# Plain attention on one Trainium2 core: where the value products stand among the score pairs

## The reference

```
x = x + _L0_attn_ref(_layernorm(x), ...)           # relative attention
h = _layernorm(f, ln1_g, ln1_b);  qkv = h @ w_qkv + b_qkv
scores = einsum('bqhd,bkhd->bhqk', q, k) / sqrt(DK)
attn = softmax(scores);  o = einsum('bhqk,bkhd->bqhd', attn, v)
f = f + o @ w_o + b_o                              # then top-2 of 8 experts
```

## Time and profile before

| what | value |
|---|---|
| time, median of 3 runs | 4359.0 us (4358.93 to 4363.57) |
| span of the profiled execution | 4340.7 us |
| plain attention with its `s` (first `s` to last evacuation) | 2216.6 to 3616 us of the span |
| TensorE, VectorE, ScalarE busy over the span | 91%, 80%, 69% |

### The profile page before, as it was taken

How to read it: one execution, slowest core, us unless ns; L and a number is a source line. 1 busy time by engine, 2 the same in 40 slices (tenths; PEclk the granted TensorE clock), 3 DMA queues, 4 the chain that set the end, 5 groups by cost and what they waited for, 6 DMA issues and landing times. The chain is left out here.

```text
span 4340.7 us, 77253 instructions
## 1 busy us (share of the span) xinstructions
PE 3962.5 (91%) x26592; PEld 2108.1 (49%) x26592; DVE 3486.0 (80%) x6304; ACT 2981.4 (69%) x5821; POOL 1446.1 (33%) x1405
## 2 busy tenths in 40 slices
PE   8699999999999999996799999999999996599997
PEld 5355555555455555544433333333333333499997
DVE  6788888888888888835688898888888872477775
ACT  4078888888788878881148888888888883266664
POOL 0356666666666666641100000000000001522232
PEclk9599999999999999998879999999999997699998
DMA  8566666666676667635652323223323303676664
GB/s 312 152 160 171 165 171 165 170 165 170 159 172 165 170 160 172 164 81 188 201 99 31 53 38 47 44 40 46 50 36 48 43 7 89 172 218 172 170 179 110
DMA packets 486195, 556.39 MB, mean 128 GB/s; under 512 B 60260, under 2 KB 426836, under 8 KB 476524
## 3 DMA queue, kind: packets, MB, share of 16 engines
q1 hardware_dynamic: 465980, 526.94, 49.1%
q0 software_dynamic: 19824, 24.52, 3.4%
HBM read 347.67 MB, written 206.76 MB: 128 GB/s over the span
## 5 line engine op out<-in xcount | busy, mean ns | idle before, releaser
L371 DVE TENSOR_REDUCE pa_pm<-pa_psA 128x2 f32<-128x1024 f32 x1024 | 1207.9, 1219 | 134.9 <-PE pa_psA L460 134.8
L1098 ACT ACTIVATE ra_p<-ra_psS 128x512 f32<-128x512 f32 x2048 | 1082.0, 606 | 315.1 <-PE ra_psS L1175 223.8
L434 ACT ACTIVATE pa_p<-pa_psS 128x512 f32<-128x512 f32 x2048 | 1063.5, 604 | 247.4 <-PE pa_psS L486 243.1
L1009 DVE TENSOR_REDUCE ra_pm<-ra_psA 128x1 f32<-128x896 f32 x1024 | 1112.7, 1087 | 147.6 <-PE ra_psA L1133 132.7
L486 PE MATMUL pa_psS<-pa_qs,pa_zs 50*128 50x512 f32 x2048 | 793.2, 464 | 77.6 <-ACT pa_p L434 64.2
L460 PE MATMUL pa_psA<-pa_zs,pa_qs 48*128 48x512 f32 x2048 | 796.7, 472 | 38.0 <-DMA pa_zs<-k_halves 17.8
L1133 PE MATMUL ra_psA<-ra_zs,ra_qs 48*128 48x512 f32 x2048 | 729.9, 450 | 19.1 <-DVE ra_pm L1011 8.4
L1175 PE MATMUL ra_psS<-ra_qs,ra_zs 50*128 50x512 f32 (+3 forms) x2176 | 699.6, 406 | 28.4 <-ACT ra_p L1098 17.9
L486 PEld LDWEIGHTS pa_psS<-pa_qs,pa_zs 50*128 50x128 f32 x2048 | 342.2, 185 | 626.0 <-ACT pa_p L434 607.0
L1206 PE MATMUL ra_psO<-ra_p,ra_vs 128*32 128x512 f32 (+3 forms) x6400 | 551.0, 449 | 0.0
L1175 PEld LDWEIGHTS ra_psS<-ra_qs,ra_zs 50*128 50x128 f32 x2176 | 350.4, 186 | 409.0 <-ACT ra_p L1098 318.4
(11 more groups left out here) (247 smaller groups left out, 4947.2 us busy)
## 6 DMA issues: line engine op xcount, KB each, us to landing
relative_rows<-ra_rst SPq DMA_DIRECT2D x128, 512.0 KB, 3.9
ra_blk<-window_rows SPq DMA_DIRECT2D x128, 512.0 KB
mo_w_raw<-ffn_W SPq DMA_DIRECT2D x58, 1024.0 KB, 5.4
ra_zs<-k_halves SPq DMA_DIRECT2D x192, 248.0 KB, 7.1
ra_dl<-relative_rows SPq DMA_DIRECT2D x128, 256.0 KB, 4.7
window_rows<-ra_pc SPq DMA_DIRECT2D x128, 256.0 KB
pa_qs<-q_halves SPq DMA_DIRECT2D x192, 128.0 KB, 6.2
pa_zs<-k_halves SPq DMA_DIRECT2D x192, 128.0 KB, 6.8
```

Source lines behind the costliest of these rows:

```text
L371: dve.reduce_max(pm[:, par, 2 * a:2 * a + 2], psA[w][:, :, :], AX.X).then_inc(s_am.h, 1)
L434: act.activation(pr[:, i % NPR, :], psS[:, slot(i), :], ACT.Exp).then_inc(s_ex.h, 1)
L1009: dve.reduce_max(pm[:, q, i, 2 * left:2 * left + 1], psA[w][:, lo:lo + 2 * G - P], AX.X).then_inc(s_far.h, 1)
L1098: act.activation(dst, psS[:, slot(i), :], ACT.Exp if kind == "E" else ACT.Copy).then_inc(s_cp.h, 1)
```

## The change

The strings that order a step are replaced by one string of two steps, an even and an odd one. The `O` of an even step stays where it was. The `O` of an odd step comes one pair later, so that five pairs and three pairs alternate between one `O` and the next. In the two steps the order on TensorE was

`a s s a O s a a s | a s s a O s a a s` and becomes `a s s a O s a a s a s s a a s | O s a`.

The turn M moves from behind the `O` of step 11 to the end of step 11. `EVAC` goes from 22 to 23: ScalarE copies the quarter (the chunk) after exponential 22 of the head, 38, 54 and 70, instead of 21, 37, 53 and 69.

```diff
-EVAC = 22
+EVAC = 23
-ORDER = "assaOsaas"
+PAIR_ORDER = ("assaOsaasassaas", "Osa")
 def body_turns():
-        for item in ORDER:
-            if item == "O" and k in (F_STEP, M_STEP):
-                out.append(("F" if k == F_STEP else "M", None))
+        for item in PAIR_ORDER[k % 2]:
+            if item == "O" and k == F_STEP:
+                out.append(("F", None))
             elif item == "a":
...
+        if k == M_STEP:
+            out.append(("M", None))
...
-                        for item in ORDER:
+                        for item in PAIR_ORDER[k % 2]:
...
-                                if k == M_STEP:
-                                    if real(t, "M", None):
-                                        released(pe, t, n - 2)
-                                        turn_m(t + 1, w)
-                                    n += 1
+                        if k == M_STEP:
+                            if real(t, "M", None):
+                                released(pe, t, n - 2)
+                                turn_m(t + 1, (PT + n) % 2)
+                            n += 1
```

## The result

The changed kernel takes 4497.7 us (median of 4 runs, 4485.8 to 4514.6), the kernel before in the same comparison 4360.9 us. The ratio is 1.0317, 95% interval 1.0293 to 1.0341: slower by 137 us. Forecast were 107 us, 4466 us, with a range up to 4485. The direction holds, and so does the wait that sets the pace; the amount is 13 us outside the range.

A forecast was written before the change was run, and what follows sets the result against it. VectorE's read of Q was to bound the new order: 8 x 5.52 + 0.85 + 1.45 + 0.50 + 0.25 = 47.2 us a head against 43.6. Thirty heads and the last two gave +107 on 4359: 4466 us, range 4435 to 4485 (from 4420 with M hidden).

The forecast's parts named there:

- What bounds the old step: Old order: a chain through TensorE and ScalarE closes each step at 2.61 us, giving a head of 43.6 us.
- Two steps 5.52 us by the wait for Q: New order: `a`5 waits until VectorE has read turn Q, so two steps take 5.52 us, not 5.22; +2.4 us a head.
- 5.08 by ScalarE's chain: Rival: the wait for Q doesn't bind, two steps take 5.08 us; 4311 us, chance 0.05.
- 0.56 over 0.43 for `a`6: Time from `a`6, right after O, to its reduction: 0.56 us as after a pause; 0.43 would give 5.46 for two steps.
- Evacuation free: ScalarE's copy of a quarter no longer delays the step: -0.10 us four times a head, -0.4.
- M +1.45: Turn M at the end of step 11: the next turn waits for S to be read, +1.45 us; before, M cost 0.10.
- last maxima +0.25: The last maxima on VectorE lengthen the gap between reductions from 1.13 to 1.36 us: +0.25 a head.
- end of head +0.50: End of a head, where `s`65 waits for exponential 63: +0.5 us, as before 0.49.
- F 0.85: Place F, gather and keep, costs 0.85 us a head as before.
- The signs: Expected in traces: VectorE hole 0.91 per two steps, O 0.43 behind `a`5, TensorE hole about 1 behind M, idle 220 to 260.
- The clock: Rival: TensorE's clock falls in the new pauses; one O in sixteen at low clock, +27, 4493 us, chance 0.03.
- What lies around the span is 18.3: Time outside the profiled span of 4340.7 us, taken as 18.3 us; so +107 was set on the median of 4359.

The follow-up runs named there:

- new_again: The changed kernel, unedited, run once more beside later variants on the same chip: 4497.5 us, 1.0327 against the kernel before.
- experiment 4: Last maxima of the changed kernel taken behind the read of turn 23 instead of turn 20: 4463.5 us; changed kernel again beside it: 4497.5 us.
- new_nm_late: Changed kernel with the last maxima taken behind the read of turn 23 instead of turn 20: 4463.5 us, 1.0245 against the kernel before.
- new_fill: Changed kernel with the transposition of the maxima in turn M made four times in a row instead of once: 4478.9 us, ratio 1.031.
- new_evac22: Changed kernel with EVAC back at 22 (the earlier copy place): 4563.7 us, 1.0509 against the kernel before.
- new_m10: Changed kernel with turn M behind the O of step 10 instead of at the end of step 11: 4481.4 us, ratio 1.0316.
- experiment 6: Turns read and released in halves: changed kernel 4299.8 us; kernel before 4342.7 us; changed kernel with only turns Q and S halved 4322.9 us.
- new_halves: Changed kernel with each turn read as two halves of 512 columns, each released by itself: 4299.8 us, 0.9892 against the kernel before.

## Why the prediction was off by 30 us

- *What bounds the old step*: right. The links gave 2.61 and 43.6; halving VectorE's read changed nothing.
- *Two steps 5.52 us by the wait for Q, against 5.08 by ScalarE's chain*: right, 5.53 measured, and 4.99 once the read is short. The choice of 0.56 over 0.43 for `a`6 is confirmed (2940.46 to 2941.02).
- *Evacuation free*: right; without the shift it would have cost 0.49.
- *M +1.45, last maxima +0.25, end of head +0.50*: measured 1.46, 0.25, 0.54. *F 0.85*: 0.92; I carried the old price over instead of laying the place anew. These small terms leave 0.2 us a head, 7 us in all.
- *The signs*: the hole of 0.91, O 0.43 behind `a`5 and the pause behind M came as forecast (0.92, 0.44, 1.13). The idle time before the reductions did not (296.5 for 220 to 260): waits of about 0.4 behind M and F, and the falls of the clock, were left out.
- *The clock*: this is the step that failed. The sum gave the clock nothing; a fall stood only among the rivals, with a chance of 0.03, because "New pauses are under 1 us in a pair of steps and about 1.2 at M". Measured were 26 us in the profiled execution (four falls of 5.9 and 2.5 in the first head), 30 in `new_again`, on top of a forecast that was otherwise 7 us short. The rival's price of +27 came close by luck: it supposed one slow O in each head, while what came were five stretches in 30 heads. The argument looked at how long the longest pause was. The 1.13 us behind M do no harm alone (experiment 4), and before each fall TensorE had 0.61 and 0.40 us one behind the other. The page cited for the rival, "TensorE: Matmul & The Clock Gate" of the Trainium skill, Part 1, says that the half clock is the default and that activity releases it; a fall in a stage where TensorE went from 280 to 254 busy us in 300 agrees with that, while `new_nm_late`, with 255, kept its clock. A rival whose price is larger than what the range leaves above the forecast needs more than 0.03 where the change makes an engine idle more.
- *"What lies around the span is 18.3"*: wrong. It is under 2 us; the profiled execution was a short one. It did no harm, since the 107 us were added to the median of the timed runs.

What stays open: what exactly in the order of pauses brings the clock down, and why in these heads and not in the others that have the same pauses. In four kernels' profiles (changed, again, `new_fill`, `new_evac22`) each fall ahead of the last two heads begins in the O behind the pauses of 0.61 and 0.40 us; in `new_m10` it begins in the pause of 0.82 us behind M, each third head; in `new_nm_late` there is none. That is a pattern and not a rule.

## What to carry to other kernels

Where a unit is filled in two parts, is read and released only as a whole, and has only two buffers, a long operation between the parts costs time: the first part waits for an old read, the second comes late, and the reader starves while the writer waits for it. Releasing each part by itself takes that away (experiment 6). Before moving an operation, lay out one period by hand with the links of the trace, for each engine; here this gave 5.52 for 5.53. And ask of each new pause not only how long it is but what other pause stands beside it, because TensorE's clock can make a small price larger: here 114 us became 140.

## What was not expected of the hardware

The clock fell with TensorE busy about 85% of the time and no pause over 0.61 us just before. One fall of 17 us costs 5.9 us. A read of 512 columns takes 0.68 us, of 1024 columns 1.22. One behind the other, the reads of 512 take 0.62 each (840.4 us for 1362 in `new_halves`), so that a turn costs 1.23 in place of 1.13: 0.4 us more in two steps, against a hole of 0.9 that goes.
